# Four-layer kernel: tile places, fetches and scatters of the first layer and the routing of the last layer are put in another order

## The reference, cut to what matters

```
xn = layernorm(x);  x = x + attn_l(xn) + ffn_l(xn)          # l = 0..3

# first layer, attn: a state-space scan, 64 heads of 8 channels, chunks of Q = 128 tokens
a = dt * A;  cum = cumsum(a) inside a chunk
M[i,j] = (C_i . B_j) * exp(cum_i - cum_j) * dt_j   (j <= i);   Yd = M @ xs
states = sum_q exp(cum_last - cum_q) dt_q B_q xs_q;  S = S * exp(cum_last) + states
y = Yd + exp(cum) * (C @ S_before) + D * xs;  out = rmsnorm(y * silu(z)) @ W_out
# first layer, ffn: router over 8 experts, the best 2 of each token, and a shared expert
out = sum_{e in top2} w_e * (silu(x Wg_e) * (x Wu_e)) Wd_e  + shared(x)

# last layer, attn: token shift, r = sigmoid(mix @ Wr), vmix = sum_t decay_t v_t,
x2 = x + r * (vmix @ Wo + bo);  out = x2 + sigmoid(xc @ Wcr) * (relu(shift(xc) @ Wck)^2 @ Wcv)
# last layer, ffn: logits = x @ Wrouter + bias; best 2 of 8; expert MLP with clipped gate and up
```

## Time and profile before

| | us |
|---|---|
| median of 3 runs | 1617.82 (1613.74 to 1619.62) |
| profiled execution, its own time | 1622.43 |
| its span in the profile | 1620.6 |
| PE busy | 1323.1 (82%) |
| DVE busy | 936.6 (58%) |
| ACT busy | 534.5 (33%) |
| POOL busy | 412.4 (25%) |
| mean granted PE clock | 0.895 |

### The profile page before, as it was taken

One profiled execution on the slowest core, in us unless ns is written; L12 is line 12 of the kernel. 1 busy time (PEld: TensorE's weight loads), 2 busy tenths in 40 slices (PEclk: granted clock), 3 DMA queues, 4 the chain that ended last, 5 costly groups with the idle time before them and its releaser, 6 DMA issues. The chain is left out here.

```text
span 1620.6 us, 21650 instructions
## 1 busy us (share of the span) xinstructions
PE 1323.1 (82%) x7251; PEld 818.1 (50%) x7251; DVE 936.6 (58%) x1888; ACT 534.5 (33%) x885; POOL 412.4 (25%) x380
## 2 busy tenths in 40 slices
PE   5765988897898556999999897898556599988997
PEld 3433645555564334657666544454343364644464
DVE  6767565664646874213103489898676445567434
ACT  1454356536535530222222231333112123233311
POOL 3278224313528641200400110000015300000035
PEclk9877999998989676999999898999856698999999
DMA  9232113212213222100000230000001100111113
GB/s 357 67 90 80 43 35 107 63 40 79 83 29 107 75 66 74 39 0 1 0 0 0 105 129 1 0 1 1 1 3 65 59 20 27 33 39 56 53 49 117
DMA packets 72082, 88.86 MB, mean 55 GB/s; under 512 B 19174, under 2 KB 55334, under 8 KB 71337
## 3 DMA queue, kind: packets, MB, share of 16 engines
q1 hardware_dynamic: 65836, 70.78, 14.1%
q0 software_dynamic: 6144, 16.79, 3.3%
HBM read 61.14 MB, written 26.38 MB: 54 GB/s over the span
## 5 line engine op out<-in xcount | busy, mean ns | idle before, releaser
L398 PE MATMUL l_banks<-l_xnT,all_region_a 128*128 128x512 f32 x288 | 129.0, 601 | 0.0
L1877 PE MATMUL l_banks<-l_xnT,mid_region_c 128*128 128x512 f32 (+1 forms) x192 | 96.3, 654 | 17.5 <-DVE l_xnT L2060 17.5
L2720 POOL TENSOR_TENSOR l_rstd<-l_moments,all_neg_half 128x4 f32<-128x4 f32 x20 | 20.6, 1030 | 337.5 <-DVE l_moments L2760 337.4
L914 POOL TENSOR_TENSOR all_region_b<-all_region_b,l_lc 128x512 f32<-128x512 f32 x64 | 87.8, 1393 | 36.5 <-DMA all_region_b<-l_lc_rows 36.1
L928 POOL TENSOR_TENSOR l_rw<-l_xdt,l_decay 128x512 f32<-128x512 f32 x64 | 71.8, 1152 | 63.9 <-DVE l_xdt L1171 63.9
L1191 DVE TENSOR_TENSOR all_region_b<-all_region_b,l_cbd 128x512 f32<-128x512 f32 x64 | 77.6, 1213 | 16.3 <-ACT all_region_b L746 12.2
L398 PEld LDWEIGHTS l_banks<-l_xnT,all_region_a 128*128 128x128 f32 x288 | 54.5, 193 | 61.5 <-issue 60.3
L398 PE MATMUL l_banks<-all_region_b,l_xp 128*32 128x32 f32 x2048 | 32.3, 208 | 62.9 <-DVE all_region_b L1191 62.8
L746 ACT ACTIVATE all_region_b<-all_region_b 128x512 f32<-128x512 f32 x64 | 69.0, 1079 | 14.6 <-PE l_banks L398 10.4
L1877 PEld LDWEIGHTS l_banks<-l_xnT,mid_region_c 128*128 128x128 f32 (+1 forms) x192 | 37.7, 202 | 68.3 <-issue 49.6
L398 PE MATMUL l_banks<-all_region_a,all_xa 128*128 x234 | 68.8, 418 | 1.3 <-DVEq L1040 0.4
(11 more groups left out here) (442 smaller groups left out, 2883.6 us busy)
## 6 DMA issues: line engine op xcount, KB each, us to landing
all_region_b<-l_lc_rows SPq DMA_DIRECT2D x256, 64.0 KB, 2.1
all_xa<-slots_in SPq DMA_DIRECT2D x39, 128.0 KB, 2.1
slots_out<-all_xa SPq DMA_DIRECT2D x39, 128.0 KB, 2.0
mid_vector_rows<-slots_in SPq DMA_DIRECT2D x39, 128.0 KB, 2.1
slots_out<-all_region_a SPq DMA_DIRECT2D x39, 128.0 KB, 1.7
slots_in<-l_xp SPq DMA_DIRECT2D x4, 1024.0 KB, 12.7
all_region_a<-l_gate_up SPq DMA_DIRECT2D x1, 4096.0 KB, 14.4
all_x<-x SPq DMA_DIRECT2D x4, 512.0 KB, 5.6
```

The costliest lines, as they stand in the source:

```text
L398: return nc.tensor.matmul(out, lhsT, rhs, start=start, stop=stop, **kw)
L914: nc.gpsimd.tensor_tensor(bc[:, k, :, :], bc[:, k, :, :], spread(lc[:, c, heads], 1, BLK), ALU.subtract).then_inc(dd_ready.sem, 1)
L1877: return nc.tensor.matmul(out, lhsT, rhs, start=start, stop=stop)
L2720: nc.gpsimd.tensor_tensor(rstd[:, :], moments[:, :, 1], mem.neg_half[:, 0:GT], ALU.pow).then_inc(rstd_ready.sem, 1)
```

## The change: what it does

Four things in the first layer. (1) The last chunk (2,3) gets no tile steps any more: 32 places, and 10 of them hold two steps, (0,3,2), (1,0,1), (1,1,0), (1,1,3), (1,2,2), (1,3,1), (2,0,0), (2,0,3), (2,1,2), (2,2,1). (2) The fetches: tiles 2 to 7 in chunk (2,3), ahead of `out_scale(2,2)` and `gate(2,3)`; tiles 0, 1 and 8 to 11 before the first differences of group 3, 12 to 15 behind them; none in group 3's chunks. (3) The scatters: 4 tiles before group 0's first differences, 2 after its first `weigh`, then 1 and 2 in chunk 0, 2 and 2 in chunk 1, 3 in chunk 2. (4) The last chunk's `out_stats` stands before `quantise(1)`.

In the last layer the statistics of the first norm get own buffers and a step `mx`; ACT copies both halves of `turn_x` into two buffers by turns; the ranking is one step over all 16 tiles; `nl 0`, `bias` and `nm 0` come behind the dispatch and `scatter 0`.

```
-    places = [(g, c, k) for g in range(GROUPS - 1) for c in range(NCH) for k in range(PIECES) if (g, c) >= (0, 3)]
-    places = sorted(places + [places[4 * i + 6] for i in range(STEPS - len(places))])
+    places = [(g, c, k) for g in range(GROUPS - 1) for c in range(NCH) for k in range(PIECES)
+              if (0, 3) <= (g, c) < (GROUPS - 2, NCH - 1)]
+    places = sorted(places + [places[3 * i + 2] for i in range(STEPS - len(places))])
...
             if t == 0:
+                jobs.wait_filled(pool, 0, ("xT", GROUPS - 1, DK - 1))
+            if t == GT // 2:
                 for i in range(2):
                     pool.wait_ge(moe.oe_out[i], 16 * ((MOE_TILES - i + 1) // 2))
-                jobs.wait_filled(pool, 0, ("xT", GROUPS - 1, DK - 1))
...
-        late = {0: ((8, 9), (10, 11)), 1: ((12, 13), (14, 15))}
+        late = {0: ((6,), (7, 8)), 1: ((9, 10), (11, 12)), 2: ((13, 14, 15), ())}
         for g in range(GROUPS):
             if g == 0:
-                for t in range(2 * GT):
+                for t in range(GT):
                     scatter(t)
             if g == GROUPS - 1:
-                for t in range(2 * GT):
+                for t in (*range(GT // 2), *range(2 * GT, 3 * GT)):
                     fetch(t)
             differences(g, 0)
             if g == GROUPS - 1:
-                for t in range(2 * GT, 3 * GT):
+                for t in range(3 * GT, 4 * GT):
                     fetch(t)
             weigh(g, 0)
+            if g == 0:
+                for t in range(GT, GT + 2):
+                    scatter(t)
             for c in range(NCH):
                 ahead, behind = late.get(c, ((), ())) if g == 0 else ((), ())
                 if c + 1 < NCH:
                     differences(g, c + 1)
                     for t in ahead:
                         scatter(t)
                     weigh(g, c + 1)
+                elif g == GROUPS - 2:
+                    for t in range(GT // 2, 2 * GT):
+                        fetch(t)
                 if c > 0:
                     out_scale(g, c - 1)
                 gate(g, c)
                 for t in behind:
                     scatter(t)
-                if g == GROUPS - 1:
-                    for t in ((12, 13), (14,), (15,), ())[c]:
-                        fetch(t)
...
+        out_stats(GROUPS - 1, NCH - 1)
         quantise(1)
-        out_stats(GROUPS - 1, NCH - 1)
...
-    PLAN = [("nx", 0), ("nx", 1), ("consts", 0), ("turn_x", 0), ("nx", 2), ("route", 0), ("turn_x", 1), ("bias", 0),
-            ("nx", 3), ("route", 1), ("turn_x", 2), ("ml", 0), ("nl", 0), ("route", 2), ("turn_x", 3), ("nm", 0),
-            ("route", 3), ("dispatch", 0), ("scatter", 0), ("turn_l", 0), ("ml", 1), ("nl", 1), ("mix", 0),
-            ("scatter", 1), ("nm", 1), ("turn_l", 1), ("scatter", 2), ("scatter", 3), ("weights", 0), ("mix", 1),
-            ("scatter", 4), ("scatter", 5), ("time_row", 0), ("scale", 0), ("scatter", 6), ("turn", 0), ("no", 0),
-            ("scatter", 7), ("nc", 0), ("tx", 0)]
+    PLAN = [("mx", 0), ("mx", 1), ("nx", 0), ("turn_x", 0), ("mx", 2), ("nx", 1), ("turn_x", 1), ("route", 0),
+            ("mx", 3), ("consts", 0), ("nx", 2), ("turn_x", 2), ("route", 1), ("nx", 3), ("turn_x", 3), ("route", 2),
+            ("route", 3), ("rank", 0), ("ml", 0), ("dispatch", 0), ("scatter", 0), ("nl", 0), ("bias", 0), ("nm", 0),
+            ("scatter", 1), ("turn_l", 0), ("ml", 1), ("nl", 1), ("mix", 0), ("scatter", 2), ("nm", 1), ("scatter", 3),
+            ("turn_l", 1), ("weights", 0), ("mix", 1), ("scatter", 4), ("scatter", 5), ("time_row", 0), ("scale", 0),
+            ("scatter", 6), ("turn", 0), ("no", 0), ("scatter", 7), ("nc", 0), ("tx", 0)]
...
+    rows_T = [xnT, mixT]
...
         def turn_x(g):                                   # ScalarE; VectorE's turn_x is gone
-            jobs.wait_filled(act, 0, ("xnT", g, 1))
-            if g > 0:
-                jobs.wait_filled(act, 0, ("route", g - 1))
-            nc.scalar.activation(xnT[:, 1, :], jobs.bank(("xnT", g, 1)), ACT.Copy).then_inc(turned_act.sem, 1)
-            jobs.free(act.drain(), ("xnT", g, 1))
+            if g > 1:
+                jobs.wait_filled(act, 0, ("route", g - 2))
+            for k, turned in enumerate((turned_0, turned_1)):
+                jobs.wait_filled(act, 0, ("xnT", g, k))
+                nc.scalar.activation(rows_T[g % 2][:, k, :], jobs.bank(("xnT", g, k)), ACT.Copy).then_inc(turned.sem, 1)
+                jobs.free(act.drain(), ("xnT", g, k))
...
+        def rank_all(_):                                 # VectorE: what route(g) did per group, on TILES at once
+            nc.vector.tensor_reduce(lmax[:, :], lg[:, :, :], AX.X, ALU.max)
+            a, c = spread(lg[:, :, :], 2, N_EXP), spread(lg[:, :, :], 3, N_EXP)
+            nc.vector.tensor_tensor(gt, a, c, ALU.is_gt)
+            nc.vector.tensor_tensor(eq, a, c, ALU.is_equal)
+            nc.vector.tensor_tensor(lg[:, :, :], lg[:, :, :], spread(lmax[:, :], 2, N_EXP), ALU.subtract)
+            nc.vector.tensor_tensor(eq, eq, spread(mem.lower[:, :, :], 1, TILES), ALU.mult)
+            nc.vector.tensor_tensor(gt, gt, eq, ALU.add)
+            nc.vector.tensor_reduce(rank[:, :, :], gt, AX.X, ALU.add)
+            nc.vector.tensor_scalar(chosen[:, :, :], rank[:, :, :], 2.0, None, ALU.is_lt)
+            nc.vector.tensor_scalar(first[:, :, :], rank[:, :, :], 1.0, None, ALU.is_lt)
```

More of the change, by code:

```diff
@@ L2278, in layer3 @@
     rc = sb("rc", [P, GT, DIM])
-    lmax = sb("lmax", [P, GT])
-    pairs = GT * N_EXP * N_EXP
-    gt, eq = [junk[:, i * pairs:(i + 1) * pairs].rearrange("p (t e f) -> p t e f", e=N_EXP, f=N_EXP) for i in range(2)]
+    lmax = sb("lmax", [P, TILES])
+    moments_x = sb("moments_x", [P, TILES, 2])
+    rstd_x = sb("rstd_x", [P, TILES])
+    pairs = TILES * N_EXP * N_EXP
+    gt, eq = [b[:, 0:pairs].rearrange("p (t e f) -> p t e f", e=N_EXP, f=N_EXP)
+              for b in (rc[:, :, :].rearrange("p t d -> p (t d)"), xcT[:, :, :].rearrange("p k n -> p (k n)"))]
+    rows_T = [xnT, mixT]
     vm = sb("vm", [P, HALVES, DK])
@@ L2367, in layer3 @@
     jobs = Jobs(mem, banks, 1, [(n, i % 8) for i, n in enumerate(names)])
-    measured = {"nx": "nx", "ml": "nl", "nm": "nm", "turn": "turn", "nc": "nc"}
+    measured = {"mx": "nx", "ml": "nl", "nm": "nm", "turn": "turn", "nc": "nc"}
     norm_steps = [(measured[step], n) for step, n in PLAN if step in measured]
@@ L2468, in dispatch @@
             pe.wait_ge(consts_ready, 1)
-            pe.wait_ge(ranked.sem, ranked.done(0, GROUPS - 1))
+            pe.wait_ge(ranked.sem, 1)
             jobs.wait_room(pe, 0, "counts")
@@ L2722, in power, with power_x @@
             return one
+        def power_x(g):
+            tiles = slice(g * GT, (g + 1) * GT)
+            pool.wait_ge(moments_ready.sem, moments_ready.done(0, norm_at["nx", g]))
+            nc.gpsimd.tensor_tensor(rstd_x[:, tiles], moments_x[:, tiles, 1], mem.neg_half[:, 0:GT], ALU.pow).then_inc(
+                rstd_ready.sem, 1)
         def scatter(g):
@@ L2777, in normalise, with measure_x @@
             return last
-        def norm_x(g):
-            measure(lambda t: x[:, g * GT + t, :], 1e-5)
-            normalise(norm_at["nx", g], lambda t: x[:, g * GT + t, :], lambda t: xn[:, g * GT + t, :]).then_inc(
-                normed_ready.sem, 1)
-        def turn_x(g):
-            jobs.wait_filled(dve, 0, ("xnT", g, 0))
-            nc.vector.tensor_copy(xnT[:, 0, :], jobs.bank(("xnT", g, 0))).then_inc(turned_dve.sem, 1)
-            jobs.free(dve.drain(), ("xnT", g, 0))
+        def measure_x(g):
+            tiles = range(g * GT, (g + 1) * GT)
+            for t in tiles:
+                nc.vector.bn_stats(stats[:, t - g * GT, :], x[:, t, :])
+            dve.drain()
+            for t in tiles:
+                nc.vector.bn_aggr(moments_x[:, t, :], stats[:, t - g * GT, :])
+            dve.drain()
+            var = moments_x[:, g * GT:(g + 1) * GT, 1]
+            nc.vector.tensor_scalar(var, var, 1e-5, None, ALU.add).then_inc(moments_ready.sem, 1)
@@ L2789, in route @@
+        def norm_x(g):
+            dve.wait_ge(rstd_ready.sem, rstd_ready.done(0, norm_at["nx", g]))
+            for t in range(g * GT, (g + 1) * GT):
+                last = nc.vector.tensor_scalar(xn[:, t, :], x[:, t, :], moments_x[:, t, 0:1], rstd_x[:, t:t + 1],
+                                               ALU.subtract, ALU.mult)
+            last.then_inc(normed_ready.sem, 1)
         def route(g):
-            tiles = slice(g * GT, (g + 1) * GT)
-            l4 = lg[:, tiles, :]
             jobs.wait_filled(dve, 0, ("route", g))
-            last = nc.vector.tensor_tensor(l4, jobs.bank(("route", g))[:, 0:GT * N_EXP].rearrange(
-                "p (t e) -> p t e", e=N_EXP), spread(row("router_bias"), 1, GT), ALU.add)
+            last = nc.vector.tensor_tensor(lg[:, g * GT:(g + 1) * GT, :], jobs.bank(("route", g))[
```

(1 more changed line is left out.)

44 lines of the change are left out of this document (17 added, 27 removed).

## The result

| | before | after |
|---|---|---|
| median, runs on the same chip | 1616.32 us (1613.74 to 1619.62) | 1600.48 us (1598.73 to 1602.50) |
| ratio | | 0.9901, 95% interval 0.9878 to 0.9925 |
| span of the profile | 1620.6 us | 1597.0 us |
| PE, DVE busy | 1323.1, 936.6 us | 1313.2, 910.8 us |
| mean granted PE clock | 0.895 | 0.909 |

The change makes the kernel about 15.8 us faster. The forecast was -6.4, 1611 us, with a range from 1600 to 1624. The measured time lies 0.5 us inside that range and outside the 1605 to 1617 given for the forecast itself. It is near rivals A and B, but B's reason turned out wrong and A's explains at most a part.

What follows compares the result with a forecast made beforehand. PE, busy 82% of the span, was taken to set most of it. Terms -9.5 + 8.6 - 5.3 - 2.5 - 0.7 + 3.0 = -6.4 took the median from 1617.8 to 1611 us; range 1600 to 1624.

Steps and rivals of the forecast that it cites:

- rival A: Cheap doubles: seven new places cost only PE's 1.95 each, net +2.0 for +8.6; 1604.8 us in all; chance 0.15.
- Rival B: Last layer keeps its 4.5 us gain from the earlier first send; sum -13.9, 1603.9 us; chance 0.10.
- scatters, to gate (0,2): Group 0: spread sends let DVE in between POOL's batches, next of chunk 3 soon follows weigh; -9.5, bounds -2.5 and -12.
- places, to gate (2,2): Tile steps: ten doubled pieces cost 32.0 where six cost 23.4; net +8.6, bounds -3.9 and +15.6.
- chunk (2,3) and start of group 3, to gate (3,0): Chunk without its four steps -5.3; fewer fetches before group 3's first weigh -2.0.
- later chunks of group 3, to gate (3,3): POOL loses four tiles' fetches there: -0.5; bound 0 if a chunk's DVE product is blocked anyway.
- from there to the next layer: End of first layer: out_stats ahead of quantise removes out_add's wait for POOL; -0.7, bounds 0 and -0.8.
- last layer, whole: First send 4.5 earlier, but POOL's longer waits and one more power make the last send later: +3.0, bounds -4.5 and +6.
- Rival C: Group 0: DVE stays blocked, or the lock frees it anyway; -2.5 for -9.5, sum +0.6, 1618.4 us; chance 0.15.
- Rival D: Second steps cost 5.0 at each new place, queued on ACT; +26.6 for +8.6, sum +11.6, 1629.4 us; chance 0.12.
- signs of being wrong: Doubles averaging over 4.6 or under 2, fetches waiting for the last step's results, or last layer's first send not earlier.

Runs made afterwards that it cites:

- set 3: Third set of runs, on one chip: kernel before again (0.9998), changed kernel again (0.9897, 1600.27 us) and two edits of the changed kernel (0.9958 and 0.9856).
- first pair: Profiles of the kernel before and the changed kernel from the first measurement: spans 1620.6 and 1597.0 us, medians 1616.32 and 1600.48 us.
- the last kernel: Changed kernel with the last layer's sends ahead of the norms and the channel mixing's first turn one expert tile later: 0.9856, 1593.50 us.
- set 2: Second set, on another chip: four edits of the changed kernel (statistics back, paired doubles, sends ahead, old places): 1.0015, 0.9998, 0.9973, 0.9973; changed kernel itself not run.

## Why the prediction came out as it did

In us, from gate to gate; the pair of set 3 is the kernel before and the changed one on one chip.

| step | predicted | first pair | pair of set 3 | undone by itself |
|---|---|---|---|---|
| scatters, to gate (0,2) | -9.5 | -8.9 | -4.5 | 7.5 slower |
| places, to gate (2,2) | +8.6 | +6.8 | +4.8 | |
| chunk (2,3) and start of group 3, to gate (3,0) | -5.3 - 2.0 = -7.3 | -7.9 | -4.9 | |
| later chunks of group 3, to gate (3,3) | -0.5 | -7.4 | -6.4 | fetches of 12 to 15: 6.4 slower |
| from there to the next layer | -0.7 | -2.8 | -2.9 | 2.8 in traces |
| layers 2 and 3 | 0 | -2.2 | -0.7 | |
| last layer, whole | +3.0 | -1.2 | +0.2 | 1.3 faster |
| sum | -6.4 | -23.6 | -14.3 | |

What was undone by itself adds up to 7.5 + 6.4 + 2.8 - 1.3 = 15.4 of the 15.8 measured. The second and third rows together were forecast at +1.3 and came to -1.1 and -0.1: the new places and the move of the fetches ahead of group 3's chunks, taken together, moved next to nothing. They belong together all the same: with the new places and the twelve fetches left behind, the kernel was 10.2 slower.

The direction was forecast rightly. That the time lies inside the range, by 0.5 us, is partly luck: 9.4 us were missing, and the range that held them was drawn for cheap doubles and an early last layer, not for what brought them.

**The later chunks of group 3 are the term that failed.** The prediction priced them at -0.5, with the bound that a DVE product there "is blocked anyway". It is blocked, but not for the same time. POOL and DVE from gate (3,0) on in the kernel before, set 3:

```profile
540.59 1.27 POOL L937 TENSOR_TENSOR l_yg<-l_yg,l_zs 128x512 f32<-128x512 f32 x1 [3.87 <-DVE l_yg L1231]
...
547.40 4.93 POOL L914 TENSOR_TENSOR all_region_b<-all_region_b,l_lc 128x512 f32<-128x512 f32 x4
```
```profile
547.26 5.92 DVE L1264 SCALAR_TENSOR_TENSOR all_x<-all_xa,l_share,all_x 128x256 f32<-128x256 f32 x2
```

and of the changed kernel:

```profile
536.01 1.27 POOL L938 TENSOR_TENSOR l_yg<-l_yg,l_zs 128x512 f32<-128x512 f32 x1 [4.17 <-DVE l_yg L1236]
537.23 6.23 POOL L915 TENSOR_TENSOR all_region_b<-all_region_b,l_lc 128x512 f32<-128x512 f32 x4
```
```profile
539.61 2.73 DVE L1269 SCALAR_TENSOR_TENSOR all_x<-all_xa,l_share,all_x 128x256 f32<-128x256 f32 x2
```

Before, four fetches stand behind the gate, the subtractions start when DVE starts its add of two SBUF operands, and POOL runs them without a gap (4.93) while DVE stands still: 5.92 for 1.05. Without the fetches the subtractions start 5.6 us sooner after the gate (1.2 for 6.8), DVE's other work falls between them (6.23 for the four), and the add takes 2.73. That is 3.2 us, and the distance of gates (3,0) and (3,1) falls by 3.0 (27.8 to 24.8), that of (3,1) and (3,2) by 3.4. The experiment that put the fetches back brought back the 5.95, and gates (3,0) and (3,3) were 76.0 apart for 69.6: 6.4 in the trace as in the medians.

**The boundary** was priced by DVE's wait of 0.66. What the next layer starts behind is POOL, whose last root came 2.8 earlier. The chain of that wait is in no row of the two; it shows only in the constant 6.44.

**The scatters** worked as written: six sends between POOL's batches let DVE in, and `next` follows `weigh` at once. POOL's own `weigh(0,3)` ended only 1.2 earlier (157.88 for 159.04; I had 2.5), so the rest is DVE's. The size was 2 too large against the experiment. I had the last send land at 154; DVE stood until 156.57 for it. And the kernel before differs by 4 us in this stretch between its own two profiles (gate (0,0) at 121.21 and 117.17, with a granted clock of 0.71 and 0.85 from 90 to 125 us).

**Doubles and chunk (2,3).** By the net of +6.8 and +4.8, and with my 3.9 for each of the old six, a double costs (23.4 + 6.8)/10 = 3.0 or 2.8, an estimate, where I had 3.2 and rival A 2.5 on average. A single double does not decide: (2,2), with its double at k = 1, is 3.7 longer, but two at k = 0 and 3 make (1,1) only 4.4 longer than a chunk without (25.3 for 20.9), 2.2 each, which is near A's price. A is neither the whole cause nor ruled out as a part of it. By the measure of the earlier trace rows, first piece to out-projection, chunk (2,3) lost 11.7 - 6.1 = 5.6 in set 3 for the 5.3 forecast. But its fetches were not quite hidden: gate (2,3) came 3.5 late (14.2 for 17.7, above), and PE waited 2.02 behind it in the first profile. Between gates the kernel before itself took 22.7 and 19.6 for the chunk; the granted clock from 465 to 485 us was 0.78 and 1.00, so the two columns of the third row differ at least in part for a reason outside the change.

**The last layer.** The waits of 1.9, 3.9, 1.0 and 1.1 measured 1.57, 4.10, 1.34 and 1.18; first send -5.4 for -4.5, so the first tile came at +1.8 for +3. That a late first tile is worth its whole delay was too much: the layer as a whole changed by -1.2 and +0.2. Rival B's gain did not come by itself; the last kernel shows what it needed, sends that do not stand behind the norms in POOL's list.

Rival C is out: DVE was let in (5.62 for 9.72), and the old scatters were 7.5 slower, not 2.5. Rival D needed 5.0 a double. Of the signs of being wrong none came: doubles between 2 and 4.6, no wait of the fetches for the last step's results (the first starts 0.17 behind the gate), the first send earlier.

## What to carry over

An engine that loses a collision should be priced by when the two operations start, not by that they collide: moving a few DMA issues shifted POOL's batch against DVE's add and was worth 6.4 us, where I had given it 0.5. Ask of each list what its last instruction releases, on every engine, before pricing an edit at a layer's end by the wait of one. When a list is tied to several engines, the engine that issues can be sent ahead of its norms. And before a wait in a trace is given to the order of the instructions, compare what fed it with an undisturbed execution: the 6.16 us behind the second tile belonged to set 2's chip, not to the list. A gate that a list of issues holds up no longer marks the end of its chunk: read such a stretch across it.

## What the runs showed of the hardware

A DVE operation with both operands in SBUF waited for eight POOL tensor operations in a row in group 0 (9.72 us, in three executions: both profiles of the kernel before and the one with the old scatters) and for four in group 3 (5.92). When sends stood behind the first four it waited for those four alone (5.62); when the batch had begun 2.4 us before it, it took 2.73. In the long waits DVE's row begins 0.12 and 0.14 us before POOL's first (149.87 and 149.99, 547.26 and 547.40). The Trainium skill, "SBUF — State Buffer", section "SBUF: two separate sides", says that whoever starts first holds the shared ports for the whole instruction and the other is blocked. By that the loser would wait for one instruction, here 1.0 to 1.2 us (4.16/4 and 4.93/4, an estimate); the measurement decides, and why DVE waited for whole batches is open.

On one chip PE issued 64 small products with pauses of 0.2 to 1.8 us that no semaphore explains, over 13 us, while twelve indirect fetches went out, and ACT and DVE stood still beside it. During the last layer's sends PE waited 5.1 to 5.4 us for ACT's copy of `toT` instead of 1.62, as DVE had begun the step before it late. Both went with POOL's indirect DMAs in time, and the kernel without fetches in (2,3) had no pause there; the cause is open. The Trainium skill, "Runtime: NRT & Kernel Launch", section "Instruction fetch mechanics", says that crossing a block of the instruction buffer costs one step of a DMA queue and is mostly hidden. No run here shows whether fetching instructions is what paused.
